# Second cross attention: y narrowed to 64 numbers in two column halves and widened again, in place of a folded 128 by 128 matrix

## What is computed

```
q_hk  = (hidden_q @ Wq.T).reshape(b, s, H, K)
q_big = einsum('bshk,hkq->bshq', q_hk, w_kc_q)      # 384 numbers a head and token
...                                                  # q_big is rotated: q*cos + rotate_half(q)*sin
q_r   = einsum('bshq,hqr->bhsr', q_rot, W_qr)        # 64 numbers
k_r   = einsum('bld,hdr->bhlr', kv_rope, W_kr)
scores = einsum('bhsr,bhlr->bhsl', q_r, k_r)
```

## Time and profile before

| | |
|---|---|
| median of 3 runs | 2045.65 us (2041.42 to 2046.24) |
| the profiled execution | 2043.4 us, of which its span 2041.6 us |
| TensorE busy | 1916.4 us, 94% of the span |
| DVE, ACT, POOL busy | 64%, 45%, 50% |
| queries of the second cross attention | from 843 to 1093 us of the span |

### The profile page before, as it was taken

How to read it: one execution, slowest core, us unless ns; L and a number is a source line. 1 busy time by engine, 2 the same in 40 slices (tenths; PEclk the granted TensorE clock), 3 DMA queues, 4 the chain that set the end, 5 groups by cost and what they waited for, 6 DMA issues and landing times. The chain is left out here.

```text
span 2041.6 us, 30196 instructions
## 1 busy us (share of the span) xinstructions
PE 1916.4 (94%) x9274; PEld 1432.8 (70%) x9274; DVE 1308.6 (64%) x2881; ACT 919.8 (45%) x2258; POOL 1016.8 (50%) x926
## 2 busy tenths in 40 slices
PE   7988999999999999999997899989997999999996
PEld 6857999886588844577674799977764666566664
DVE  4578887466651122477776788858865666677665
ACT  2555555233412100244444555535434665666662
POOL 1248885112252200377777788667402455566662
PEclk9999999999999999999999999999996999999998
DMA  5551332200211100012225133320035999999997
GB/s 184 201 202 55 109 106 67 84 1 1 104 61 42 43 8 0 20 61 85 94 81 193 52 104 100 109 70 1 15 130 186 311 338 328 248 233 237 233 237 195
DMA packets 104957, 251.55 MB, mean 123 GB/s; under 512 B 14800, under 2 KB 40912, under 8 KB 96304
## 3 DMA queue, kind: packets, MB, share of 16 engines
q1 hardware_dynamic: 82224, 196.02, 29.0%
q0 software_dynamic: 21136, 51.11, 10.8%
q10 hardware_dynamic: 1440, 2.49, 0.3%
HBM read 279.44 MB, written 55.07 MB: 164 GB/s over the span
## 5 line engine op out<-in xcount | busy, mean ns | idle before, releaser
L99 PE MATMUL banks<-L1f_w,L1f_xT 128*128 x760 | 263.2, 490 | 0.9 <-ACT L1f_xT L2781 0.9
L2999 POOL DMA_INDIRECT moe_sums<-L1f_y,L1f_row x94 | 149.6, 1592 | 171.6 <-DVE L1f_is_who L2868 93.0
L99 PEld LDWEIGHTS banks<-L1f_w,L1f_xT 128*128 128x128 f32 x760 | 138.1, 192 | 78.1 <-issue 3.3
L160 POOL TENSOR_TENSOR rstd<-rstd,power 128x1 f32<-128x1 f32 x48 | 32.0, 666 | 221.8 <-DVE rstd L154 221.8
L3007 POOL DMA_INDIRECT L1f_xg<-moe_rows,L1f_row x95 | 107.9, 1136 | 60.3 <-DVE L1f_spare L2859 25.2
L99 PE MATMUL banks<-L0f_down,L0f_z 128*128 128x512 f32 x256 | 111.1, 592 | 1.5 <-DVE L0f_z L2241 1.5
L2702 PE MATMUL banks<-L1f_w,L1f_zT 128*128 x190 | 98.3, 599 | 4.6 <-DVE L1f_z_rest L2839 4.6
L99 PE MATMUL banks<-L0f_hT_hi,L0f_ug_hi 128*128 128x512 f32 x256 | 100.0, 391 | 0.0
L99 PE MATMUL banks<-L0f_hT_lo,L0f_ug_hi 128*128 128x512 f32 x256 | 99.6, 389 | 0.0
L99 PE MATMUL banks<-L0f_hT_hi,L0f_ug_lo 128*128 128x512 f32 x256 | 99.6, 389 | 0.0
L2313 POOL TENSOR_TENSOR L0f_ug_lo<-w,L0f_ug_hi 128x512 fp32r<-128x512 f32 x32 | 42.9, 1353 | 113.1 <-ACT L0f_ug_hi L2217 113.1
(11 more groups left out here) (439 smaller groups left out, 5893.5 us busy)
## 6 DMA issues: line engine op xcount, KB each, us to landing
L1f_w<-in_experts SPq DMA_DIRECT2D x95, 1280.0 KB
L1f_laid<-moe_counts SPq DMA_DIRECT2D x59, 512.0 KB, 6.3
w<-in_L1x_heads SPq DMA_DIRECT2D x16, 704.0 KB, 4.0
L0x_q<-L0x_far SPq DMA_DIRECT2D x20, 512.0 KB
L1x_q<-L1x_far SPq DMA_DIRECT2D x20, 512.0 KB
w<-in_L0x_heads SPq DMA_DIRECT2D x8, 1216.0 KB, 6.2
L0x_far<-L0x_away_far SPq DMA_DIRECT2D x8, 1024.0 KB
w<-in_wug SPq DMA_DIRECT2D x8, 1024.0 KB, 4.9
```

The lines of the kernel that those rows point to most:

```text
L99: ins = pe.e.matmul(out, w, m, start=first and n == 0, stop=last and n == len(pairs) - 1)
L160: pool.e.tensor_tensor(self.rstd[:, i:i + 1], self.rstd[:, i:i + 1], self.power[:, 0:1], ALU.pow).then_inc(self.rstd_set.sem, 1)
L2999: pool.e.indirect_dma_start(self.sums[j % 2][:, :], bass.IndirectOffsetOnAxis(ap=self.row[:, j:j + 1], axis=0), self.y[j % self.NY][:], No ...
```

## The change

`u` and its fold go. N(k) multiplies y by W_qr directly (weights 128x64), in two column halves of 256 tokens: half 0 writes partitions 0 to 63 of bank 7, half 1 partitions 64 to 127. ACT copies both halves as high part into rows 0 to 63 of `narrow_halves` (`narrow_hi`), DVE subtracts into rows 64 to 127 (`narrow_lo`). A new step **S(k)**, `spread_narrow`, multiplies the stacked 128 rows by W_kr, which the host lays down twice, once for each half of the rows, and which ACT and POOL split into high and low (`kr_high`, `kr_low`, once a head): two fp32r matmuls of 128x512. S(k) writes the first of the banks of W(k+1). The query is kept from there. A head's weights are 1216 instead of 1408 columns, and the last signal of a slot is now `narrowed` of the head's second unit, that is N(2h+1).

```diff
-L1_PACK = {"wq": KD * XK, "kcq": DCQ, "qr": DCQ, "kr": DC}
+L1_PACK = {"wq": KD * XK, "kcq": DCQ, "qr": QC * RR, "kr": DC}
...
-                                      [(self.u_made, h + 1), (self.ws_hi, h + 1), (self.wq_lo, h + 1),
-                                       (self.kcq_lo, h + 1)]) for h in range(XH)]
+                                      [(self.narrowed, 2 * h + 2), (self.ws_hi, h + 1), (self.wq_lo, h + 1),
+                                       (self.kcq_lo, h + 1), (self.kr_hi, h + 1), (self.kr_lo, h + 1)]) for h in range(XH)]
...
+    def out_of(self, k):
+
+        return self.wide(k + 1)
...
-        for k in range(n + 1):
+        for k in range(n + 2):
             if k < n:
                 self.widen(pe, k)
-                if k + 2 < n:
-                    self.ask(pe, k + 2)
-            if k >= 1:
+            if k >= 2:
+                self.spread_narrow(pe, k - 2)
+            if k + 2 < n:
+                self.ask(pe, k + 2)
+            if 0 < k <= n:
                 self.narrow(pe, k - 1)
-            if k < n and k % 2 == 0:
-                self.fold_u(pe, k // 2)
...
     def widen(self, pe, k):
...
+            self.kept_units(pe, k - 2)
...
     def narrow(self, pe, k):
         h, t = self.units[k]
-        pe.wait_ge(self.u_set, h + 1)
-        self.kept_units(pe, k)
+        self.head_w[h].landed(pe)
+        pe.wait_ge(self.m_hi, 2 * k)
+        pe.wait_ge(self.m_lo, 2 * k)
+        half = BANK // 2
         for c in range(QC):
             pe.wait_ge((self.pair_set, self.pair_set, self.rest_set)[c], k + 1)
-            ins = pe.e.matmul(self.sh.psum(self.SMALL), self.u[h % 2][:, c, :], self.y[k % 3][:, c, :], start=c == 0,
-                              stop=c == QC - 1)
+            for i in range(2):
+                ins = pe.e.matmul(self.sh.psum(self.SMALL)[i * RR:(i + 1) * RR, 0:half], self.w(h, "qr")[:, c * RR:(c + 1) * RR],
+                                  self.y[k % 3][:, c, i * half:(i + 1) * half], start=c == 0, stop=c == QC - 1)
         ins.then_inc(self.narrowed.sem, 1)
+
+    def spread_narrow(self, pe, k):
+        h, t = self.units[k]
+        pe.wait_ge(self.kr_hi, h + 1)
+        pe.wait_ge(self.kr_lo, h + 1)
+        pe.wait_ge(self.m_hi, 2 * k + 2)
+        pe.wait_ge(self.m_lo, 2 * k + 2)
+        if k + 1 < len(self.units):
+            pe.wait_ge(self.sin_set, 2 * (k + 2))
+            pe.wait_ge(self.cos_set, 2 * (k + 1) + 1)
+        self.kept_units(pe, k - 1)
+        accumulate(pe, self.out_of(k), [(part[:], self.narrow_halves[:]) for part in self.kr[h % 2]]).then_inc(self.spread.sem, 1)
```

More of the change, by code:

```diff
@@ L1038, in __init__ @@
             self.away_far, self.away_next = sb("away_far", [P, 2, self.HALF, BANK], F32R), sb("away_next", [P, 2, BANK], F32R)
-            self.u = [sb(f"u{i}", [P, QC, DC]) for i in range(2)]
+            self.kr = [tuple(sb(f"kr_{v}{i}", [P, DC], F32R) for v in ("hi", "lo")) for i in range(2)]
+            self.narrow_halves = sb("narrow_halves", [P, BANK], F32R)
             self.qh = [tuple(sb(f"qh_{v}{i}", [P, BANK], F32R) for v in ("hi", "lo")) for i in range(2)]
@@ L1109, in fold_ready @@
             pe.wait_ge(self.swapped, 2 * n)
+        elif h == 1:
+            self.kept_units(pe, n - 1)
         elif h == 3:
[L1111 removed]
+            pe.wait_ge(self.qh_hi, n)
+            pe.wait_ge(self.qh_lo, n)
     def kept_units(self, eng, n):
@@ L1172, in ask @@
             cut(self.ws[h % 2], slice(None), slice(c * XK, (c + 1) * XK)), self.tokens(c, t))]).then_inc(self.asked.sem, 1)
[L1174 to L1182, removed]
     def widen(self, pe, k):
@@ L1238, in scalar @@
             if k % 2 == 0:
-                self.keep_u(act, k // 2)
+                self.kr_high(act, k // 2)
             if k >= 1:
-                self.keep_query(act, k - 1)
+                self.narrow_hi(act, k - 1)
+        self.keep_query(act, n - 2)
+        self.narrow_hi(act, n - 1)
         self.keep_query(act, n - 1)
@@ L1246, in keep_query, with kr_high, narrow_hi @@
         h, t = self.units[k]
-        act.wait_ge(self.narrowed, k + 1)
[L1248 to L1254, removed]
+        act.wait_ge(self.spread, k + 1)
+        self.keep_query_hi(act, h, t, self.out_of(k))
+    def kr_high(self, act, h):
+        self.head_w[h].landed(act)
+        act.wait_ge(self.spread, 2 * (h - 1))
+        act.e.copy(self.kr[h % 2][0][:], self.w(h, "kr")).then_inc(self.kr_hi.sem, 1)
+    def narrow_hi(self, act, k):
+        act.wait_ge(self.narrowed, k + 1)
+        act.wait_ge(self.spread, k)
+        half, out = BANK // 2, self.narrow_halves
+        for i in range(2):
+            act.e.copy(out[0:RR, i * half:(i + 1) * half],
+                       self.sh.psum(self.SMALL)[i * RR:(i + 1) * RR, 0:half]).then_inc(self.m_hi.sem, 1)
     def split_weights_hi(self, act, h):
@@ L1285, in vector @@
         self.query_low(dve, n - 2)
+        self.narrow_lo(dve, n - 1)
         self.query_low(dve, n - 1)
@@ L1290, in query_low, with narrow_lo @@
         h, t = self.units[k]
-        self.keep_query_lo(dve, h, t, self.sh.psum(self.SMALL), self.query_sets(h, t))
+        self.keep_query_lo(dve, h, t, self.out_of(k), self.query_sets(h, t))
+    def narrow_lo(self, dve, k):
+        dve.wait_ge(self.m_hi, 2 * k + 2)
+        half, out = BANK // 2, self.narrow_halves
+        for i in range(2):
+            at = slice(i * half, (i + 1) * half)
+            dve.e.tensor_tensor(out[RR:P, at], self.sh.psum(self.SMALL)[i * RR:(i + 1) * RR, 0:half], out[0:RR, at],
+                                ALU.subtract).then_inc(self.m_lo.sem, 1)
     def rows_lo(self, dve, i):
@@ L1344, in gpsimd @@
                 self.wq_low(pool, k // 2 + 2)
+            if k % 2 == 0:
+                self.kr_low(pool, k // 2)
             pool.wait_ge(self.sin_set, 2 * k + 2)
@@ L1353, in gpsimd, with kr_low @@
         self.pool_attention(pool)
+    def kr_low(self, pool, h):
+        hi, lo = self.kr[h % 2]
+        pool.wait_ge(self.kr_hi, h + 1)
+        pool.e.tensor_tensor(lo[:], self.w(h, "kr"), hi[:], ALU.subtract).then_inc(self.kr_lo.sem, 1)
     def wq_low(self, pool, h):
```

20 lines of the change are left out of this document (12 added, 8 removed).

## The result

The changed kernel takes 2017.91 us (median of 4 runs, 2016.38 to 2018.99), the kernel before, run beside it, 2043.54 us (4 runs). The ratio is 0.9875 with a 95% interval of 0.9854 to 0.9895. Two later series with other runs of both gave 0.9883 (0.9866 to 0.9901) and 0.9889 (0.9867 to 0.9912). The profiled execution took 2016.38 us, its span 2014.3.

A forecast was written before the change was run, and what follows sets the result against it. TensorE's own work was taken to bound the query stage. 13 x (15.41 - 13.68) = 22.5, plus 4.5 at the start and 2.8 at the end, 29.8 us off 2043.4, gives 2013.6; predicted 2015 us, range 2006 to 2037.

The forecast's parts named there:

- halves side by side and TensorE bound: Query stage: N's halves overlap in two strips and TensorE's work sets the time, 2008 to 2021 us, chance 0.60.
- the prediction's own signs of being wrong: N of 2.5 or more, PE waiting for L363 or the low part, L1285 for the load, or later attention not simply shifting.
- The 0.06 us per queued pass: Issue time per pass in N, read from self attention rows; the second half starts two issues later, 0.12 us.
- the 1.2 us that program order was said to cost: If N's passes kept program order in start and end, N is 1.69 us, 1.2 us more over 13 pairs.
- The iteration: TensorE's W, S, A and N: 2.06 + 0.46 + 2.72 + 1.60 = 6.84 us, a pair 13.68 against 15.41.
- x = 0: Odd iterations: `kcq_low`, held to the pair add's end at 9.0, ends at 9.4; x later makes the pair x longer.
- The margin of 0.02 us: The bank W(k+2) waits for is ready at 6.77 plus 0.05 us, TensorE at 6.84.
- The start: W(1) need not wait for U(0), so W(3) starts at 861.2, not 865.6: 4.5 us gained.
- The weights' slots: Load issued once N(2h+1) ends arrives by 4.3 us, ACT wants it at 4.4: cost zero, almost no cover.
- The rival's 13 us: Late weights: every load a microsecond late costs up to 13 us, 2028 us, chance 0.09.
- The end: W(29) to the first fold takes 23.9 us instead of 26.7, a gain of 2.8 though S(31) is exposed.
- Halves in series: N's halves run one after the other: N 2.74 us, a pair 15.96, 2048 us, chance 0.07.

The follow-up runs named there:

- ends_packed: Changed kernel with fillings and folds in TensorE's last waits, folds 0 to 3 kept early, `kcq_low` ahead of the low part in iterations 1 and 25: 2013.71 us.
- kcq_first: Changed kernel with `kcq_low` ahead of the low part of the narrowed halves on DVE in odd iterations: 2036.56 us, ratio 0.9963 to the kernel before.
- wide_load_after: Changed kernel with each load of a head's weights made 1280 KB in place of 608: 2028.40 us, ratio 0.9918 to the kernel before.
- one_block: Changed kernel with the two column halves of N undone, one block of 512 columns: 2053.90 us, ratio 1.0039 to the kernel before.

## Why the prediction was right, and where it wasn't

The forecast case, halves side by side and TensorE bound, was the right one, and 2015 lies 3 us below 2017.9. The sum promised 29.8 us in the stage, though, and the stage gave 20.9 (22.2 in the two later profiles); the medians say 21 to 26. So the nearness is in part luck: the profiled run's 2016.38 owes 6.4 us to the rest of the program, which no step forecast. The 8.9 us that are missing in the stage are about 1.5 at the start, 3.4 in the pairs and 4.1 at the end. Two of the prediction's own signs of being wrong showed, in small: TensorE waited for L363 (4.1 us in four waits) and L1285 for the load (0.7 in two).

- **N, right by two errors.** The second half was to start 0.12 behind the first; it starts 0.01 behind. An edge was to cost 0.09; both together cost 0.35. 1.60 was forecast, 1.64 measured. The 0.06 us per queued pass, on which the 0.12 rested, has no support in the blocks above. And the 1.2 us that program order was said to cost over 13 pairs should have been 2.3: 13 pairs have 26 narrowings of 0.09 each.
- **The iteration.** 6.84 forecast, 6.90 and 6.98 measured; N has 0.04 of it, and in even iterations the step from S's first matmul to its second is 0.27 where 0.23 was counted. 13 pairs at 13.87 in place of 13.68 are 2.5 us. A size, not a mechanism: TensorE was busy without a wait in the regular pairs, clock 1.00.
- **`kcq_low`.** Forecast: held to the add's end and 0.41 behind it, about 1.0 long, x = 0. Measured 0.87, ending 0.43 behind. The margin of 0.02 us was as narrow as forecast: beside `ends_packed`, where ACT's split came 0.24 late in one iteration, `kcq_low` ended 0.22 later and the next iteration took 7.19 in place of 6.97. `kcq_first` shows what the place in DVE's order is worth, 1.8 us a pair. The Trainium skill, GPSIMD Engine Reference, "Specifications", has the shared SBUF interfaces for this; the 2.78 us beside the pair add and the 0.42 of `narrow_lo`, which reads PSUM, agree.
- **The start, 3.0 and not 4.5.** The step that failed took W(3) to be free of `kcq_low`. In iteration 1 the pair add starts 0.55 us ahead of `kcq_low` and not 1.96 as later (timeline of the changed kernel, below), so `kcq_low` was held for 2.30 us and W(3) waited 1.24. The prediction worked out the odd iteration once, from its steady state. With it moved ahead, `kcq_first` and `ends_packed` have the 1.3 us back.

```profile
853.75 2.42 POOL L1387 TENSOR_TENSOR L1x_y<-L1x_y,L1x_turn_part 128x1024 f32<-128x1024 f32 x1
...
854.30 2.30 DVE L1368 TENSOR_TENSOR L1x_ws_lo<-w,L1x_ws_hi 128x384 fp32r<-128x384 f32 x1
```

- **The weights' slots.** Forecast: cost zero with almost no cover. Measured: 13 loads of 608 KB, two late by 0.3 and 0.4, each issued 0.4 ahead of a send (a third load so placed wasn't late); 0.9 us lost. The prediction had looked at the sends before a load and put nothing for them. "Each microsecond late costs one" is shown, "every load" is wrong: a late load covers the next. The rival's 13 us for a microsecond were near twice too many.
- **The end, -1.3 and not 2.8** (W(29) to the transpose; -0.4 and -0.2 in the two later profiles). The step that failed is the sum of 23.9 us, which took every matmul at full clock. W(31) waited for the kept query and S(31) for the low part, as forecast; with S(30), which waited too, these are 6.6 us. In this stretch TensorE ran W(31) and a part of the folds at 1.2 GHz: 1.7 and 1.7 us. `wide_load_after`, with the same waits and full clock, gains 2.1 there. The rest, 0.7, is in the waits: W(31) follows W(30) by 6.2 us where 5.8 was worked out, and from W(31) to the folds it is 11.6 in `wide_load_after` where 11.3 was.
- **Halves in series**, the slower rival, was sized at 2048 from N = 2.74; `one_block` is that case, with N = 2.91 and 2053.9.

## What to carry to other kernels

A matmul with 64 output rows cost as much here as one with 128 (0.43 us a pass in `one_block`) until its columns were dealt to two strips of the array, here output partitions 0 to 63 and 64 to 127. Do that, alternate the strips pass by pass, and count the edges of the group as a cost of their own. `kcq_low`, a DVE instruction with two SBUF inputs, ended 0.4 us behind POOL's long add wherever it started beside it. Place such an instruction to meet the add's end, or to start ahead of it, and work out the first and last rounds too: they have other offsets than the steady state. When a stage's last rounds leave the bounding engine idle, look there for the next stage's work.

## What the runs showed of the hardware that was not expected

- A strip starts passes ahead of program order: the first of half 1 together with the third of half 0, 0.48 us behind half 0's first, though six passes stood ahead of it. With eight passes a block the offset was 0.47.
- Going to a group of 64 output columns and back cost 0.35 us in sum, whether 6 or 12 passes lay between; N with 128 output columns has no such cost (2.57 us for six passes of 0.43).
- The granted clock fell to 1.2 GHz behind 1.93 or 1.94 us of idle time in four executions, and did not in a fifth behind 1.94, nor in the kernel before behind 2.38.
- The hold between DVE and POOL works both ways and alike: the instruction that starts second takes longer by what the first has still to run, less 0.12 to 0.14 us. `kcq_low`, 0.55 us alone, took up to 2.81 behind the start of a pair add and 0.62 ahead of one of POOL's starts, while POOL's instruction that started second took 1.60 for 1.28, 2.72 for 2.40, and the rest add 1.64 for 1.3.
